# Matrix products without a reader around the routing stage, and the expert words read in two parts

## The reference

```python
def _L0_ffn_ref(x, router_w, w1, w2):
    xf = x.reshape(-1, d)
    probs = jax.nn.softmax(xf @ router_w.T, axis=-1)
    topv, topi = jax.lax.top_k(probs, 2)
    topv = topv / (topv.sum(axis=-1, keepdims=True) + 1e-09)
    cw = (jax.nn.one_hot(topi, e, dtype=xf.dtype) * topv[..., None]).sum(axis=1)
    h = jax.nn.gelu(jnp.einsum('td,edh->teh', xf, w1), approximate=False)
    y = jnp.einsum('teh,ehd->ted', h, w2)
    out = jnp.einsum('te,ted->td', cw, y)

mod = (_silu(L0_c) @ L0_wmod).reshape(L0_c.shape[0], 6, 1, -1)
...
h = _layernorm(x, axis=-1) * (1 + ca) + sa
x = x + ga * _L0_attn_ref(h, L0_attn_w_qkv, L0_attn_w_out)
h = _layernorm(x, axis=-1) * (1 + cb) + sb
x = x + gb * _L0_ffn_ref(h, L0_ffn_router_w, L0_ffn_w1, L0_ffn_w2)
```

## Time and profile before

| | |
|---|---|
| median of 3 runs | 780.34 us (778.79 to 780.62) |
| the profiled execution | 778.46 us, of which the span is 776.7 us |
| TensorE busy | 713.8 us, 92% of the span |
| VectorE, ScalarE, GpSimd busy | 629.9, 572.1, 521.5 us |
| chain that ended last | TensorE 56%, GpSimd 19%, issue 12% |

### The profile page before, as it was taken

One profiled execution on the slowest core, in us unless ns is written; L12 is line 12 of the kernel. 1 busy time (PEld: TensorE's weight loads), 2 busy tenths in 40 slices (PEclk: granted clock), 3 DMA queues, 4 the chain that ended last, 5 costly groups with the idle time before them and its releaser, 6 DMA issues.

```text
span 776.7 us, 24849 instructions
## 1 busy us (share of the span) xinstructions
PE 713.8 (92%) x8105; PEld 549.3 (71%) x8105; DVE 629.9 (81%) x1494; ACT 572.1 (74%) x1108; POOL 521.5 (67%) x535
## 2 busy tenths in 40 slices
PE   8799999999999999755799999999999999999994
PEld 5467777777777777634578777777778777777772
DVE  3999999999999999668577777777777777777773
ACT  2799899999999999730476767677776767677772
POOL 4777777777777778447566666666666666666642
PEclk9999999999999999955799999999999999999998
DMA  6324344444444433110333343434434333443310
GB/s 221 96 84 130 117 130 119 137 118 133 119 140 120 140 115 108 43 54 8 95 77 69 71 72 75 73 73 79 70 74 70 76 68 76 75 72 75 73 21 1
DMA packets 52854, 69.27 MB, mean 89 GB/s; under 512 B 8864, under 2 KB 44080, under 8 KB 52736
## 3 DMA queue, kind: packets, MB, share of 16 engines
q0 software_dynamic: 18176, 27.06, 18.6%
q1 hardware_dynamic: 34560, 40.61, 17.2%
HBM read 46.50 MB, written 22.05 MB: 88 GB/s over the span
## 4 chain that ended last, share of the span: by engine, by line
PE 56%; POOL 19%; issue 12%; DVE 6%; ACT 4%; DMA 1%; POOLq 0%; ACTq 0%; DVEq 0%
PE hidden L1374 16%; PE bank L1392 15%; PE hidden L1376 8%; PE bank L1394 8%; POOL kst L842 4%; POOL h L803 4%; POOL rstd L796 4%; POOL qst L840 3%; PE hidden L1217 3%; PE bank L1217 2%; PE bank L1234 2%; ACT h L956 2%; POOL kst L833 2%; POOL mod_b L887 1%; DVE amlo L492 1%
## 5 line engine op out<-in xcount | busy, mean ns | idle before, releaser
L1374 PE MATMUL hidden<-qstT,w1hi_k 128*128 128x256 f16 x1136 | 197.4, 274 | 0.9 <-DVE qstT L683 0.7
L1376 PE MATMUL hidden<-qstT,w1lo_k 128*128 128x128 f16 x1136 | 193.1, 220 | 0.0
L1392 PE MATMUL bank<-w,amhi 128*128 x568 | 188.4, 379 | 0.1
L1394 PE MATMUL bank<-w,amlo 128*128 x568 | 154.8, 273 | 0.0
L935 POOL DMA_INDIRECT out_dram<-x,si x71 | 115.0, 1620 | 39.0 <-issue 24.9
L719 DVE TENSOR_TENSOR amlo<-am,amhi 128x512 f16<-128x512 f32 x142 | 98.3, 692 | 48.9 <-ACT am L1093 48.9
L1374 PEld LDWEIGHTS hidden<-qstT,w1hi_k 128*128 x1136 | 111.4, 98 | 14.3 <-issue 1.5
L1376 PEld LDWEIGHTS hidden<-qstT,w1lo_k 128*128 x1136 | 111.4, 98 | 0.2
L1234 PE MATMUL bank<-wq,hT 128*128 128x512 f32 (+1 forms) x256 | 100.6, 518 | 1.3 <-DVE hT L456 1.2
L1392 PEld LDWEIGHTS bank<-w,amhi 128*128 128x128 f16 x568 | 55.6, 98 | 59.9 <-issue 0.4
L1092 ACT ACTIVATE amhi<-am 128x512 f16<-128x512 f32 x142 | 88.0, 619 | 0.0
(11 more groups left out here) (213 smaller groups left out, 1781.4 us busy)
## 6 DMA issues: line engine op xcount, KB each, us to landing
stage<-in_L_ffn_w_dram SPq DMA_DIRECT2D x32, 512.0 KB, 4.4
xt<-in_L_attn_x_dram SPq DMA_DIRECT2D x32, 128.0 KB, 4.0
out_dram<-x SPq DMA_DIRECT2D x32, 128.0 KB, 3.8
ffn_rows<-h SPq DMA_DIRECT2D x32, 128.0 KB, 1.8
ffn_rows<-am SPq DMA_DIRECT2D x32, 128.0 KB, 4.2
am<-mod_rows SPq DMA_DIRECT2D x16, 128.0 KB, 4.0
mod_b<-mod_rows SPq DMA_DIRECT2D x8, 256.0 KB, 4.3
w<-in_L_wmod_dram SPq DMA_DIRECT2D x6, 256.0 KB, 4.4
```

The lines of the kernel that those rows point to most:

```text
L1374: t.matmul(dst.rearrange("p (q n) -> p q n", q=2), w1s[0][k][g][:, w_], both, start=(k == 0), stop=False)
L1376: last = t.matmul(dst[:, P:2 * P], w1s[1][k][g][:, w_], both[:, 0, :], start=False, stop=(k == KT - 1))
L1392: t.matmul(y[:, :], ghi[:, m.p, c_m], w2s[mt // 2][:, bass.ds(w_, 2 * D)], start=(mt == 0), stop=False)
L1394: last = t.matmul(y[:, D:2 * D], glo[:, m.p, c_m], w2s[mt // 2][:, bass.ds(w_, D)], start=False, stop=(mt == MT - 1))
```

## The change

It adds a helper, `keep_running(n)`, that issues n products of 128 rows by 512 columns from `qstT` into bank 5, whose result nobody reads. They stand at four places of TensorE's list: 14 in front of the first tile group, 3 in front of each of the next six groups (none in front of the last), 8 behind the table, and 14 between the read of the words and the first transposes. That is 14 + 18 + 8 + 14 = 54 products. And the nine words are no longer read at one place: one (the experts of blocks 0 to 7) is read in front of block 0, and the other eight in step 1, between the first layer of block 1 and the second layer of block 0.

```diff
+            def keep_running(n):
+
+                for _ in range(n):
+                    t.matmul(bank[5][:, :], qstT[:, 0:P], qstT[:, 0:4 * P], start=True, stop=True)
+
             for t_ in range(2 * NC):
                 g_, u = t_ // TG, t_ % TG
                 if u == 0:
+                    keep_running((14, *[3] * (2 * NC // TG - 2), 0)[g_])
                     pe.wait_ge(b_["tile"], g_ + 1)
...
+            keep_running(8)
             pe.wait_ge(a_["whi"], NC)
             pe.wait_ge(a_["wlo"], NC)
             pe.wait_ge(s_dve, marks["block_e"])
-            _, words = nc.values_load_multi_w_load_instructions(block_e[0:1, 0:TB // UC], engines=(pe.engine,), min_val=0,
-                                                                max_val=E ** UC - 1)
+
+            def digit_words(lo, hi):
+
+                _, words = nc.values_load_multi_w_load_instructions(block_e[0:1, lo:hi], engines=(pe.engine,), min_val=0,
+                                                                    max_val=E ** UC - 1)
+                return dict(enumerate(words, lo))
+
+            digits = digit_words(0, 1)
+            keep_running(14)
             xT(At(0, 0, UC))
...
                     y = bank[1 + m.p]
+                    if m.n == 0:
+                        digits.update(digit_words(1, TB // UC))
                     wait(pe, c_["yw"], m.n - 1)
```

More of the change, by code:

```diff
@@ L1350, in _ @@
             pe.wait_ge(s_dve, marks["block_e"])
-            _, words = nc.values_load_multi_w_load_instructions(block_e[0:1, 0:TB // UC], engines=(pe.engine,), min_val=0,
-                                                                max_val=E ** UC - 1)
+            def digit_words(lo, hi):
[4 more added lines that the diff above has]
+            keep_running(14)
             xT(At(0, 0, UC))
-            expert, digits = {}, dict(enumerate(words))
+            expert = {}
             def step_c(a):
```

## The result

| | before | changed |
|---|---|---|
| median of 4 runs | 779.57 us (778.48 to 780.62) | 791.13 us (790.53 to 792.39) |
| profiled execution: time, span | 778.46, 776.7 us | 790.53, 788.8 us |
| TensorE busy | 713.8 us | 733.3 us |

The ratio is 1.0131, with a 95% interval of 1.0109 to 1.0152: the changed kernel is slower by 1.3%, or 10.2 us (8.5 to 11.8 by the interval; the two medians in the table are 11.6 us apart). The direction was forecast; the size was not. I had put the sum at 6.7 us and the median at 786.2, and the measured median lies 1.1 us above the upper end of my range. The two profiled executions are 12.1 us apart: 2.2 of it arises before line 1330, in the attention stage, and 9.9 behind it.

What follows compares the result with a forecast made beforehand. TensorE, never waiting after about 386 us, passes earlier losses to the end; other engines pace routing. 0.5 + 2.4 - 0.6 + 3.4 + 1.0 = 6.7 us; 780.34 + 6.7 - 0.6 = 786.4, stated as 786.2; range 782.8 to 790.0.

Steps and rivals of the forecast that it cites:

- The 14 in front of the first group: Before the table's first group: seven idle microseconds of TensorE hide the 14 products even at the low clock; cost nothing.
- The 18 between the groups: Table stage, three products before each of six groups: +0.5 us, ends 0 and +5.4, with the clock mostly high.
- C: Table becomes the bound: clock falls before the first group or strided products gain nothing; +9.7, 790; chance 0.11 with D.
- D: Clock not raised at all before block 0, so the products only fill time: 12.5, 792.8; chance 0.11 with C.
- The bound for a low clock throughout: Table stage: with the clock low throughout, the table would end at 372.0 plus the last product's tail, 5.7 us late.
- One word in front of block 0: Before block 0's transposes: one word in place of nine frees the sequencer at 371.15, not 373.42; -0.6 us.
- The 14 behind the word: Before block 0's transposes: products delay them 2.4 us, the gain on the words spent; ends +0.7 and +3.7.
- A high clock in block 0: First layer of block 0 and the transposes and copy: high instead of low clock gives -0.6 us, ends 0 and -1.5.
- The second read: Step 1, eight words read between layers: exposed on TensorE's sequencer with no queue ahead; +3.4 us, at least 2.9.
- The clock behind the hole: After the read in step 1: a low clock stretch may follow TensorE's standstill; +1.0 us, ends 0 and +2.5.
- A: Everything fed at the high clock, step 1's gap too short for a fall: +3.1, about 782.7; chance 0.10.
- B: Second read in step 1 hidden as well, gains stand alone, time falls: between 778.9 and 780.5; chance 0.07.

Runs made afterwards that it cites:

- the split read alone: Changed kernel with all products without a reader taken out; one word read before block 0, eight in step 1: 1.008 to the kernel before, 6.3 us slower.
- the 18 alone: Kernel before plus only three products in front of each of six tile groups, nine words read at once: 1.0055 to the kernel before, 4.3 us slower.

## Why the prediction was right or wrong

Measured on the first chip's two profiles, from line 1330 on; block 8 begins 9.9 us later, and after that nothing changes.

- **The 14 in front of the first group: right.** 4.95 us, no delay.
- **The 18 between the groups: wrong, the first failed step.** I took +0.5 between ends of 0 and +5.4. The table ended 3.6 us late. I had bounded the table products at the high clock by "twice as fast" and "not faster", and taken a value between the two; they are hardly faster (1.05 against 1.10 us). And I let the clock be mostly high behind the first group; it had risen at 354.0, fell at 357.4, in front of that group, and stayed at 0.50 until 364.2, through three of the eight groups. I had called that outcome a rival, C, and given it 0.11 with D. Its mechanism is what happened, and its 790 the nearest of my numbers; GpSimd's 4.24 us wait for `gi` is its sign. (The bound for a low clock throughout was also added up 0.3 us short: 355.52 + 8.80 + 7.74 is 372.06, which is 6.0 us behind 364.95 + 1.10, not 5.7.)
- **One word in front of block 0: right in kind.** The load took 0.50 us instead of 1.04. The rule I quoted from the Trainium skill ("DMA: Bandwidth & Descriptors", "Latency and other measured facts": a floor of about 600 ns) agrees better than my estimate from the nine-word row; the trace has 496 ns, below the floor it states.
- **The 14 behind the word: too dear for this profile.** I took 2.4 us in all, the word included. They met the high clock, and the transposes came 0.5 us behind VectorE's part, where it was 0.7 before: -0.2 in place of +2.4. Together with the late table the transposes came 3.4 us late, where I had 0.5 + 2.4 = 2.9. That this came out near is luck: the two errors cancelled. On chip 10 the same place is at +5.4.
- **A high clock in block 0: right.** From block 0 to block 1 it was 4.27 us against 4.63, and from the transposes to block 0 1.06 against 1.28: 0.6 us, as said. The first half of block 0 gained 0.65 (2.06 against 2.71), because the sequencer sets its pace. But the second half and the step to block 1 lost 0.30 (2.21 against 1.91): before, the sequencer had got ahead during the slow half, and the pairs of the second then came every 0.165 us at the high clock. That loss was not in my sum.
- **The second read: right in mechanism, too cheap.** Predicted 3.4, measured 4.2. The missing part is the load of eight words, 1.96 us and not 1.04; where nine words from word 0 on were read in its place, the hole was 3.4.
- **The clock behind the hole: the second failed step.** I took +1.0, up to 2.5. Second layer of block 0 to block 2: 5.5 us against 2.8, so +2.7, and a little in block 2. I argued that dense layers on both sides might keep the clock; in every profiled run with the eight-word read it fell, for 3.4 or 6.8 us.

The sum by what was measured: 3.4 - 0.6 + 4.2 + 2.8 = 9.8, against 6.7. Rivals A and B fall with the split read alone. D did not come. The parts were added up from one profile of each kernel on the first chip; what the other chips confirm of it is the late table (4.3 us for the 18 alone) and the second read (6.3 us for the split alone).

What I could not settle: why the table products gain nothing from the clock, and the other chips' stalls. For the first there are two readings. Their columns are read with a stride; and so are their weights, whose load takes 0.143 to 0.148 us at either clock, a little more than the time from one product to the next. The second is nearer to the rows. I tried no other layout, so neither is shown.

## What to carry to other kernels

Work without a reader is sure to be free only in front of a wait that is longer than that work at the low clock. Between steps that another engine hands over every 1.4 us, it costs what it makes the step longer than that. A register read in the middle of this dense stage cost its whole length, and the long ones the clock behind it too: look up how far the sequencer is ahead at that very place, not elsewhere in the loop. Before work is added to raise the clock, look whether the stretch behind it gets shorter at the high clock at all: the table's products did not, and block 0 gained 0.35 us net. And look whether the machine of an experiment has a wait of its own that swallows the term in question.

## What the runs showed of the hardware that I had not expected

- A read of eight words from word 1 on loads in 1.95 to 1.96 us in all six profiled runs that have it; nine from word 0 on take 1.04, or 0.87 in step 1; one word takes 0.49 to 0.50 in front of block 0 and 0.30 to 0.31 in the dense stage.
- Eight products of 72 strided columns with strided weights take 1.05 us at 2.4 GHz and 1.10 at 1.2 GHz, and each of their weight loads 0.143 to 0.148 at either, while one of 512 plain columns halves, from 0.43 to 0.22.
- The same program is 1% slower on three other chips (787.0 to 787.4 against 779.6 us), with single stalls of VectorE and ScalarE that no instruction of the core explains, and that end 13.2 to 13.4 us after the table's end in most of the profiles there. The ratio of the change was the same within its interval on the first chip and on chip 10, 1.0131 and 1.0124.
